# Slot lists in three tables (2, 6 and 8 experts), the last shared products moved behind the second list, fewer gathers ahead of the first scatter

## What is computed

```python
scores = jax.nn.sigmoid(h @ gate_w.T)                 # 2048 tokens x 16 experts
cap = math.ceil(T / E * TOP_K)                        # 256 tokens for each expert
topk_score, topk_ids = jax.lax.top_k(scores.T, cap)
xin = h[topk_ids]
up = jnp.einsum('ecd,efd->ecf', xin, up_w) + up_b[:, None, :]
g = jnp.einsum('ecd,efd->ecf', xin, gw) + gb[:, None, :]
eo = jax.nn.silu(g) * up
eo = jnp.einsum('ecf,edf->ecd', eo, down_w) + down_b[:, None, :]
flat = (eo * topk_score[..., None]).reshape(-1, Dm)
out = jnp.zeros_like(h).at[topk_ids.reshape(-1)].add(flat)
shared = jax.nn.silu(x @ sh_gate_w.T) * (x @ sh_up_w.T) @ sh_down_w.T   # every token
return out + shared
```

## Time and profile before

| | |
|---|---|
| three runs | 214.91 us median, 213.57 to 215.64 |
| the profiled execution, its own time | 213.9 us |
| its span in the trace | 211.9 us |
| PE / DVE / ACT / POOL busy | 85% / 61% / 42% / 57% |
| up to 56.7 us: wavelet, attention, router | PE 51.3, DVE 48.5, POOL 20.9 us busy |
| 56.7 to 83.3: search | PE 23.9, DVE 22.2, POOL 13.7 |
| 83.3 to 97.7: masks to the first gather | PE 11.5, DVE 11.8, POOL 4.5 |
| 97.7 to 115.8: the gathers ahead | PE 17.2, DVE 10.7, POOL 13.9 |
| 115.8 to 154.3: scatters with two gathers each | PE 37.0, DVE 17.4, POOL 31.2 |
| 154.3 to 186.9: scatters with one gather each | PE 31.7, DVE 14.7, POOL 25.0 |
| 186.9 to 211.9: last scatters | PE 8.2, DVE 4.3, POOL 12.4 |

### The profile page before, as it was taken

How to read it: one execution, slowest core, us unless ns; L and a number is a source line. 1 busy time by engine, 2 the same in 40 slices (tenths; PEclk the granted TensorE clock), 3 DMA queues, 4 the chain that set the end, 5 groups by cost and what they waited for, 6 DMA issues and landing times.

```text
span 211.9 us, 3612 instructions
## 1 busy us (share of the span) xinstructions
PE 180.6 (85%) x1198; PEld 156.4 (74%) x1198; DVE 129.4 (61%) x431; ACT 89.9 (42%) x238; POOL 121.6 (57%) x175
## 2 busy tenths in 40 slices
PE   7879889999879898879899999998988999979000
PEld 7857779999736666649699999987977999968000
DVE  4888899999788888788544444443344444444000
ACT  0676603267886864110144444444243444434100
POOL 7510006555144567504777887887887777775550
...
DMA packets 11617, 22.19 MB, mean 105 GB/s; under 512 B 1488, under 2 KB 8784, under 8 KB 11472
## 3 DMA queue, kind: packets, MB, share of 16 engines
...
...
## 4 chain that ended last, share of the span: by engine, by line
PE 32%; DMA 19%; DVE 17%; POOL 12%; issue 10%; ACT 5%; POOLq 1%; SPq 1%; DVEq 0%; ACTq 0%
DMA out_dram<-area,rows 16%; POOL out_dram L486 8%; PE bank L1081 7%; PE bank L1342 4%; PE bank L1343 4%; DVE junk L889 4%; PE bank L1327 3%; PE bank L1036 3%; DMA x_tok<-in_x_dram 2%; POOL sh_hid L460 2%; PE bank L1234 2%; PE bank L1184 2%; ACT area L504 1%; DMA hT<-h_rows,rows 1%; DVE area L740 1%
## 5 line engine op out<-in xcount | busy, mean ns | idle before, releaser
L486 POOL DMA_INDIRECT out_dram<-area,rows x32 | 50.6, 1580 | 16.7 <-DMA out_dram<-area,rows 9.7
L1021 DVE SCALAR_TENSOR_TENSOR area<-bank,consts,sgate 128x256 f32<-128x256 f32 x64 | 30.9, 482 | 38.7 <-ACT sgate L671 38.7
L671 ACT ACTIVATE sgate<-bank,consts 128x256 f32<-128x256 f32 x64 | 30.3, 473 | 56.9 <-PE bank L1343 56.9
L1327 PEld LDWEIGHTS bank<-wT,area 128*128 128x128 f32 x256 | 38.4, 191 | 3.6 <-DVE area L1021 0.4
L1342 PE MATMUL bank<-area,wT 128*128 128x256 f32 x128 | 38.6, 383 | 2.5 <-issue 2.5
L1327 PE MATMUL bank<-wT,area 128*128 128x128 f32 x256 | 38.8, 275 | 0.2 <-DVE area L1021 0.2
L474 POOL DMA_INDIRECT hT<-h_rows,rows x32 | 32.0, 1000 | 11.4 <-issue 9.1
L1343 PE MATMUL bank<-area,wT 128*128 128x256 f32 x128 | 38.1, 379 | 0.0
L1343 PEld LDWEIGHTS bank<-area,wT 128*128 128x128 f32 x128 | 24.3, 190 | 3.3
L460 POOL TENSOR_TENSOR sh_hid<-sh_up,sgate 128x64 f32<-128x64 f32 x48 | 14.4, 336 | 15.8 <-ACT sh_up L627 12.7
L1036 PE MATMUL bank<-ident 128*128 128x128 f32 x152 | 21.5, 298 | 1.6 <-POOL ident L381 1.6
...
## 6 DMA issues: line engine op xcount, KB each, us to landing
...
hT<-h_rows,rows POOLq DMA_INDIRECT x32, 2.6
out_dram<-area,rows POOLq DMA_INDIRECT x32, 3.3
...
```

Source lines behind the costliest of these rows:

```text
L486: pool.indirect_dma_start(out=out_rows, in_=eo[:, e % 2, c, :], in_offset=None, out_offset=bass.IndirectOffsetOnAxis(ap=rows[:, g, c, k:k ...
L671: act.activation(sgate_e[:, q % SGB, :], up_bank(q)[:, CAP:2 * CAP], ACT.Silu, bias=biasT[:, 1, j, e:e + 1]).then_inc(s_sil, 1)
L1021: dve.scalar_tensor_tensor(hidden[:, e % 2, j, :], up_bank(q)[:, 0:CAP], biasT[:, 0, j, e:e + 1], sgate_e[:, q % SGB, :], ALU.add, ALU.mul ...
L1327: last = pe.matmul(bank[3 + e % 2][:, c * P:(c + 1) * P], hidden[:, e % 2, j, c * P:(c + 1) * P], wT[:, e, 2, j, :], start=(j == 0 and c = ...
```

## The change

The slot numbers are now made on PE: the two masks are turned right away, and matmuls with triangular matrices (`until`, `ahead_of`) and a bf16 identity times 4096 (`lift`) add up both prefix sums; ACT and DVE keep the two results and a maximum joins them. The tables are three, for experts 0-1, 2-7 and 8-15 (`GROUPS`). Their last steps lose the transpose: DVE multiplies the picked table by a mask (`by_x`), and one matmul with another mask (`seat`) gives the rows, which a small copy keeps. The third table's pieces are put into the expert loop (`LATER`, and `table(2)` at pair 9). The four products of the last shared group go between the tables, its DVE multiplications behind the second row list, `WARM_1` is gone, and POOL's wait for the first table's copy with its memset. `down(3)` moves from pair 5 to pair 4, and with it `add_bias(0)` and `weigh(0)` stand one pair earlier. POOL makes the new masks after its second `norm_scale`, where it waits for DVE from 11.5 to 33.1 us.

The core of the diff:

```diff
-    AHEAD = 14
-    BETWEEN = (2, 2, 2, 2, 2, 2, 1, 1, 1, 1, 1, 1, 0, 0, 0, 0)
+    AHEAD = 11
+    BETWEEN = (2, 2, 2, 2, 2, 2, 2, 2, 1, 1, 1, 1, 1, 0, 0, 0)
...
+        GROUPS = ((0, 2), (2, 6), (8, 8))
...
@@ POOL
-            pool.wait_ge(s_itTe, 1)
-            pool.memset(cnt[:, 7:8], 0.0)
...
-                if e % 8 == 0 and c == 0:
-                    pool.wait_ge(s_rows, g + 1)
+                if e == 5 and c == 0:
+                    pool.wait_ge(s_shu, SHT * (LAST + 1))
+                if c == 0:
+                    for g, (e0, _) in enumerate(GROUPS):
+                        if e == e0:
+                            pool.wait_ge(s_rows, g + 1)
...
@@ ACT
-            act.wait_ge(s_posT, 2)
-            act.copy(by_token(slot_s), slots[1]).then_inc(s_slots, 1)
+            act.wait_ge(s_maskT, 1)
+            act.copy(mask_T[:, 0, :], bank[6][:, 0:256]).then_inc(s_gtT, 1)
+            act.wait_ge(s_rank, 1)
+            act.copy(by_token(slot_a), ranks[0]).then_inc(s_slota, 1)
...
-                if j == 2 and e > 0:
+                if (q == FT + 1 or j == 2 and e > 1):
                     weigh(act, e - 1)
...
@@ DVE
+            dve.tensor_copy(mask_T[:, 1, :], bank[7][:, 0:256]).then_inc(s_eqT, 1)
...
+            link(dve.tensor_tensor(by_token(slot_s), by_token(slot_a), ranks[1], ALU.max))
+            link(dve.tensor_scalar(slot_y[:, :], slot_s[:, :], -(HI + 1) / 2, ROUND16, ALU.add, ALU.add))
...
+            def hot_lo(g, i0, i1):
+                part, digits = slot_part(1, g, i0, i1)
+                return dve.tensor_tensor(hot(lo_flat, g)[:, i0:i1, :, :], part, digits, ALU.is_equal)
...
+            def hot_hi(g, i0, i1):
+                part, digits = slot_part(0, g, i0, i1)
+                return dve.tensor_tensor(hot(hi_flat, g)[:, i0:i1, :, :], part, digits,
+                                         ALU.is_equal).then_inc(s_hot, 1)
+
+            def lay_table(g):
+
+                n = GROUPS[g][1]
+                m = HI * n
                 dve.wait_ge(s_tab, g + 1)
...
+                link(dve.tensor_reduce(itab[0:m, :], ext[0:m, 0:m].rearrange("p (b e) -> p b e", e=n), AX.X, ALU.add))
+                dve.tensor_tensor(ext[0:m, P:2 * P].rearrange("p (b x) -> p b x", x=8),
+                                  itab[0:m, :].unsqueeze(2).to_broadcast([m, HI, 8]),
+                                  by_x[n][0:m, :].unsqueeze(1).to_broadcast([m, HI, 8]), ALU.mult).then_inc(s_spreadL, 1)
 
             def slot_rows(g):
+                e0, n = GROUPS[g]
                 dve.wait_ge(s_spread, g + 1)
...
+                dve.tensor_copy(rows[:, :, e0:e0 + n],
+                                spread_of(g).rearrange("p (c e) -> p c e", c=CH)).then_inc(s_rows, 1)
...
+            link(hot_lo(0, 0, NT))
+            times_token(0, 0, NT)
+            link(dve.tensor_scalar(slot_h[:, 0, :], slot_y[:, :], HI - LIFT - ROUND16, -1.0 / HI, ALU.add, ALU.mult))
+            for half in range(2):
+                hot_hi(0, half * NT // 2, (half + 1) * NT // 2)
+            link(hot_lo(1, 0, NT))
+            lay_table(0)
             slot_rows(0)
+            times_token(1, 0, NT)
+            for half in range(2):
+                hot_hi(1, half * NT // 2, (half + 1) * NT // 2)
+            lay_table(1)
+            slot_rows(1)
             for t in range(SHT):
                 dve.wait_ge(s_shsil, SHT * LAST + t + 1)
                 dve.wait_ge(s_shu, SHT * LAST + t + 1)
                 dve.tensor_tensor(sh_hid[:, LAST % 2, t, :], bank[2 + t][:, :], sgate[:, t, :], ALU.mult).then_inc(s_lasthid, 1)
             add_shared(LAST - 1, bank[4])
-            times_token(1)
-            one_hot(one_hi, 0, 1).then_inc(s_hot, 1)
             add_shared(LAST, bank[6])
...
+            LATER = {3: (hot_lo, 0), 4: (hot_lo, 1), 5: (times_token, 0), 6: (times_token, 1),
+                     7: (hot_hi, 0), 8: (hot_hi, 1)}
...
-                if j == 1 and e > 0:
+                if (q == FT or j == 1 and e > 1):
                     add_bias(e - 1)
+                if q in LATER:
+                    piece, half = LATER[q]
+                    last = piece(2, half * NT // 2, (half + 1) * NT // 2)
...
+                if q == 9:
+                    lay_table(2)
+                if q == 12:
+                    slot_rows(2)
...
@@ PE
+            rank_base(0, 0, earlier)
+            for k in range(2):
+                pe.wait_ge((s_gtT, s_eqT)[k], 1)
...
+                pe.matmul(rank[k], lift[:, :], mask_T[:, k, :], start=False, stop=False, skip_group_check=True)
+                pe.matmul(rank[k], until[:, :], mask_T[:, k, 0:P].unsqueeze(1).to_broadcast([P, 2, P]), start=False,
+                          stop=False, skip_group_check=True)
...
             table(0)
-            turn_table(0)
+            shared_up(LAST, 0, 1)
             spread(0)
+            shared_up(LAST, 1, 0)
+            table(1)
+            spread(1)
+            shared_up(LAST, 1, 1)
             pe.wait_ge(s_shsil, SHT * (LAST + 1))
-            stay_warm(WARM_1, bank[1])
             for t in range(4):
                 shared_down(LAST, t)
...
-                if q >= LAG:
+                if q == FT:
                     down(q - LAG)
+                    down(q - 1)
+                elif q >= LAG and q != FT + 1:
+                    down(q - LAG)
+                if q == 9:
+                    table(2)
+                if q == 12:
+                    spread(2)
```

More of the change, by code:

```diff
@@ L921, in _ @@
                         keys = both
-            gt, eq, scan_gt, scan_eq = (sel[:, k, :] for k in range(4))
-            slot_gt, slot_eq = slot_f[:, 0, :], slot_f[:, 1, :]
-            dve.tensor_scalar(gt, both, found, 0.0, ALU.is_gt, ALU.add, accum_out=cnt[:, 0:1])
-            dve.tensor_scalar(eq, both, found, 0.0, ALU.is_equal, ALU.add,
-                              accum_out=cnt[:, 1:2]).then_inc(s_cnt, 1)
-            dve.wait_ge(s_cnt, len(ROUNDS) + 1)
-            dve.tensor_tensor_scan(scan_gt, gt, gt, 0.0, ALU.add, ALU.max)
@@ L1253, in _ @@
                     features_T(1 + r // 4)
-            pe.wait_ge(s_cnt, len(ROUNDS) + 1)
-            pe.matmul(bank[5][:, 510:511], earlier[:, :], cnt[:, 0:1], start=True, stop=True)
-            pe.matmul(bank[5][:, 511:512], same8_bf[:, :], cnt[:, 0:1], start=True, stop=False)
-            pe.matmul(bank[5][:, 511:512], earlier[:, :], cnt[:, 1:2], start=False, stop=True).then_inc(s_tot, 1)
+            for k in range(2):
+                pe.wait_ge(s_mask, k + 1)
+                for r in range(2):
+                    last = pe.matmul(bank[6 + k][:, r * P:(r + 1) * P], junk[:, k, r:256:2], ident_b[:, :],
+                                     start=True, stop=True)
+                last.then_inc(s_maskT, 1)
@@ L1260, in _ @@
             for t in range(4):
                 shared_down(LAST - 1, t)
-            pe.wait_ge(s_pos, 1)
-            for i in (5, 6):
-                for r in range(2):
-                    for k in range(2):
-                        last = pe.matmul(bank[i][:, r * P:(r + 1) * P], slot_f[:, k, r:256:2], ident_h[:, :],
-                                         start=(k == 0), stop=(k == 1))
-                last.then_inc(s_posT, 1)
-            for t in range(4):
-                shared_up(LAST, t // 2, t % 2)
+            shared_up(LAST, 0, 0)
@@ L1316, in _ @@
             turn_x(0)
-            spread(1)
             LAG = 2
```

200 lines of the change are left out of this document (120 added, 80 removed).

## The result

The changed kernel takes **218.36 us** (median of four executions, 217.57 to 222.06) against 214.27 for the kernel before on the same chip: a ratio of 1.0194, 95% interval 1.0145 to 1.0244. It is 2% slower, where the forecast was 213.9 in a range of 211.0 to 216.8. The span of the profiled execution is 215.8 us instead of 211.9.

The account below looks back on a forecast made before the run. POOL's fixed descriptor list was taken to bound the kernel from the first gather on; -4.95 + 2.0 + 1.95 = -1.0 gave a span of 210.9 instead of 211.9, so 213.9 us, range 211.0 to 216.8.

Parts of the forecast that it names:

- S(0): Start of expert 0's first scatter on POOL: forecast at 109.6, set by PE, with POOL waiting 2.3 us.
- S(1): Start of expert 1's first scatter: forecast at 117.25 instead of 122.20, 4.95 us earlier.
- short rows: Rival: one-hot rows of 2 and 6 elements run at half rate, loop starts 103.4, time 216.15; chance 0.07.
- POOL held by DVE's pieces: Rival: the third table's DVE pieces block POOL's descriptors, S(1) 1.3 later, time 215.2; chance 0.02.
- the list behind S(1): POOL's scatter and gather steps from expert 1 to expert 12: 66.7 us instead of 64.7.
- S(12): Start of expert 12's first scatter: forecast at 183.95, before at 186.90.
- three signs of being wrong: Loop starting at 103 or later, S(14) following by landings alone, or PE's clock below 1.00 ahead of the loop.
- The last gather: Gather now behind expert 12's scatters: 3.8 behind S(12), then 8.36 to `weigh(14)`, as `turn_x(15)` precedes expert 14's last pair.
- S(14): Start of expert 14's first scatter: forecast at 196.65, or 194.7 by the landings alone; before at 197.65.
- The clock: Rival: half-busy PE drops to 1.2 GHz ahead of the loop, costing 3 to 4.5 us, 217 to 218; chance 0.06.
- 2.0 given back: Loss behind S(1): three gathers moved between scatters, where two more pairs pay 1 us each.
- 1.95 given back: Loss at S(14), which waits for the later last gather: 196.65 instead of 194.7 by landings alone.

Follow-up runs that it names:

- e2: The kernel before with 11 gathers ahead of the first scatter and the changed kernel's spacing of the others: 218.59 us, ratio 1.0200 to before.
- e3: The changed kernel with `turn_x(15)` moved behind expert 14's last pair and its two down steps, DVE and ACT order matched: 214.32 us, ratio 1.0000 to before.
- e4: The changed kernel with 24 dummy matmuls on PE ahead of `turn_x(15)`, filling its wait for the last gather: 216.88 us, ratio 1.0103 to before.
- e5: The changed kernel with 14 gathers ahead, placed as before the change, and 56 semaphore waits at the start of PE's list: 213.78 us, ratio 0.9891 to before.
- e7: The changed kernel with `turn_x(15)` behind expert 14's last pair, 14 gathers ahead and five double-gather steps: 212.78 us, ratio 0.9864 to before.
- e11: The changed kernel with eight dummy matmuls on PE ahead of the loop and 24 ahead of `turn_x(15)`: 215.71 us, ratio 1.0018 to before.

## Why the prediction was wrong, point by point

**Right in the number.** First list (91.54 for 92.0), first gather (92.45 for 92.9), the loop's start (100.72 for 101.15), S(0) (109.80 for 109.6, POOL idle 3.33 for "over 2"), S(1) (117.54 for 117.25, idle 1.33 for 1.2). `table(2)` cost 0.89 behind pair 9 (0.9), pair 8 waited 0.29 (0.5). The 6-wide one-hot piece took 0.96 for 1536 elements (0.9), so "short rows" fell; the 2-wide one took 0.63 instead of 0.4, which PE's later start hid. "POOL held by DVE's pieces" fell too: S(1) isn't 1.3 late, though one descriptor did take 1.88 instead of 1.56 beside two pieces of 0.68. The steps of "the list behind S(1)" were right in their regular rows, and e2 confirms the term: S(12) is 66.88 behind S(1) there (66.7). None of the three signs of being wrong that the prediction names is in this trace.

**Part of it was luck.** From the start of `weigh` to its scatter the sum has 0.54 (half of `weigh`, and 0.2 for POOL to start). It took 1.25 at S(0) and 1.20 at S(1). Both came out right because `weigh(0)` and `weigh(1)` started 0.5 and 0.4 sooner than summed (108.55 for 109.06, 116.34 for 116.71).

```profile
108.55 0.68 ACT L554 ACTIVATE area<-area,hT 128x128 f32<-128x128 f32 x2
...
116.34 0.68 ACT L554 ACTIVATE area<-area,hT 128x128 f32<-128x128 f32 x2
```

**The step that failed: "The last gather".** Its mechanism was right, `turn_x(15)` ahead of expert 14's last pair, and e3 shows it. Its size was not: S(14) stood at 196.65 in the sum and came at 201.58. Of the 4.93 us, 2.13 came in with S(12), from "S(1)" and "The list behind S(1)"; 2.8 arose in the step itself.

- 2.13: S(12) was late, 0.29 from S(1) and 1.84 from the landing ahead of S(11). No term of the sum allowed for a code packet, and the rows of before show no price for it: there the packets fall where nobody waits.
- 2.24: gather to `weigh(14)` took 10.60, not 8.36. I carried a duration over from a place where PE had waited 1.11 to one where it waits 6.10, and took it as if nothing but the transfer and PE's work were in it, with PE at the clock of before. e4 measured it with the clock held: 8.25. So the clock is the term that was put at nothing here.
- 0.61: from `weigh`'s start to its scatter 1.15, not the 0.54 that I counted, the error that luck covered at S(0) and S(1); no scatter of the kernel before waits for ACT longer than the 0.3 between two descriptors, so there was no row for it.
- The gather itself stood 3.75 behind S(12), as said (3.8).

**The rivals.** "The clock" had a chance of 0.06 and was put at one place, ahead of the loop. It is real there, in some executions (e3, e5, e7), and not in the profiled one; what I didn't ask is where *else* the change makes PE wait. The sum itself held the answer: gather at 183.95 + 3.8 and PE at that point of its list some us earlier, since in the kernel before it stood there from 186.91 (188.02 less 1.11) and the loop now starts sooner. The earlier trace rows show the clock falling to 0.70 where PE's list was done. The Trainium skill (TensorE: Matmul & The Clock Gate, section "Part 1: The HAM clock gate") says that idleness sets the throttle again; the trace agrees, with 0.62 and 0.50 in the windows above.

**What the change was worth.** 4.66 at S(1) was real. Behind it, where the sum has "2.0 given back" and "1.95 given back", 8.6 were given back: 2.0 and 1.9 as the sum had it, 1.84 to the late landing beside a code packet, 2.24 to the clock, 0.6 to the scatter's start. With the clock held at both places (e11) front and list together come to nothing either way.
